# Weights, shift rows and maxima moved ahead in a two-layer graph kernel

## The reference

```
def gat_layer(x, W, att_src, att_dst, bias, src, dst, heads, out_ch, concat):
    h = (x @ W.T).reshape(n, heads, out_ch)
    a_src = jnp.einsum('nhc,hc->nh', h, att_src)
    a_dst = jnp.einsum('nhc,hc->nh', h, att_dst)
    e = jax.nn.leaky_relu(a_src[src] + a_dst[dst], NEG_SLOPE)
    m = jax.ops.segment_max(e, dst, num_segments=n)
    ex = jnp.exp(e - m[dst])
    denom = jax.ops.segment_sum(ex, dst, num_segments=n)
    ... # out = sum over edges of ex / denom * h[src], then + bias

def _performer_attn(x, qkv_w, ...):          # q, k, v = x @ qkv_w
    q = _feature_map(q, w_orf); k = _feature_map(k, w_orf)
    D = jnp.einsum('bhnm,bhm->bhn', q, k_sum)[..., None] + EPSILON
    ktv = jnp.einsum('bhnm,bhnc->bhmc', k, v)
    out = jnp.einsum('bhnm,bhmc->bhnc', q, ktv) / D
    return out @ proj_w + proj_b
```

## Time and profile before

| | us |
|---|---|
| median of 3 runs | 3565.2 (3563.28 to 3566.42) |
| the profiled execution | 3567.12 |
| its span | 3565.3 |
| TensorE busy | 2986.9 (84%) |
| VectorE busy | 2337.2 (66%) |
| ScalarE busy | 1492.7 (42%) |
| GpSimd busy | 455.7 (13%) |

### The profile page before, as it was taken

One profiled execution on the slowest core, in us unless ns is written; L12 is line 12 of the kernel. 1 busy time (PEld: TensorE's weight loads), 2 busy tenths in 40 slices (PEclk: granted clock), 3 DMA queues, 4 the chain that ended last, 5 costly groups with the idle time before them and its releaser, 6 DMA issues. The chain is left out here.

```text
span 3565.3 us, 50533 instructions
## 1 busy us (share of the span) xinstructions
PE 2986.9 (84%) x18054; PEld 2541.1 (71%) x18054; DVE 2337.2 (66%) x3813; ACT 1492.7 (42%) x2551; POOL 455.7 (13%) x301
## 2 busy tenths in 40 slices
PE   8799997967999997886888599867999986886695
PEld 4699996745888997775886233356999955775694
DVE  6644443735842544996764887656888657996775
ACT  5564554213112332553142577522546413552245
POOL 0488880200000000000002300000000000000000
PEclk6899999988999998997989699978999987998897
DMA  6232223794212554224131321165111093214211
GB/s 209 58 45 32 22 14 109 221 219 97 75 47 78 178 156 120 72 64 123 42 79 31 91 49 41 45 187 132 33 56 31 26 238 105 59 45 128 63 34 45
DMA packets 252271, 311.68 MB, mean 87 GB/s; under 512 B 97911, under 2 KB 180572, under 8 KB 251438
## 3 DMA queue, kind: packets, MB, share of 16 engines
q1 hardware_dynamic: 177282, 276.77, 28.8%
q0 software_dynamic: 74784, 32.32, 5.2%
HBM read 227.47 MB, written 80.57 MB: 86 GB/s over the span
## 5 line engine op out<-in xcount | busy, mean ns | idle before, releaser
L438 POOL DMA_INDIRECT adj_d<-key_val,key_off x160 | 337.6, 2110 | 184.7 <-issue 159.6
L3067 DVE TENSOR_TENSOR expert_wgel<-expert_gel,expert_wps 128x417 f32<-128x417 f32 (+1 forms) x384 | 202.7, 584 | 56.9 <-PE expert_wps L2992 55.1
L2041 PE MATMUL gat00att_ops<-gat00att_h,gat00att_p 125*125 x1600 | 197.2, 279 | 48.6 <-DVE gat00att_p L2017 48.5
L2041 PE MATMUL gat10att_ops<-gat10att_h,gat10att_p 125*125 x1600 | 197.1, 281 | 46.2 <-DVE gat10att_p L2017 46.2
L2041 PEld LDWEIGHTS gat00att_ops<-gat00att_h,gat00att_p 125*125 125x125 f32 x1600 | 183.0, 189 | 63.0 <-issue 63.0
L2041 PEld LDWEIGHTS gat10att_ops<-gat10att_h,gat10att_p 125*125 125x125 f32 x1600 | 186.2, 194 | 57.4 <-issue 57.4
L3039 ACT ACTIVATE expert_gel<-expert_hps 128x417 f32<-128x417 f32 (+1 forms) x384 | 193.8, 519 | 56.0 <-DVE expert_wgel L3067 46.9
L606 PE MATMUL perf_wide<-y_lo,perf_qk_hi 128*128 128x416 f32 (+1 forms) x432 | 156.9, 363 | 37.2 <-DVE perf_qk_lo L795 30.3
L744 ACT ACTIVATE perf_kphi<-perf_wide,perf_lnm 125x384 f32<-125x384 f32 (+1 forms) x180 | 96.7, 630 | 180.3 <-PE perf_wide L630 173.8
L1200 PE MATMUL fc_ps<-y_lo,fc_w_hi 128*128 128x512 f32 (+1 forms) x432 | 155.3, 360 | 19.4 <-DVE fc_w_lo L1242 19.4
L1344 PE MATMUL fc_ops<-fc_w_hi,fc_x_lo 128*125 128x384 f32 x480 | 163.3, 340 | 7.2 <-DVE fc_w_lo L1392 7.2
(11 more groups left out here) (484 smaller groups left out, 8187.1 us busy)
## 6 DMA issues: line engine op xcount, KB each, us to landing
fc_w<-in_L_mix_fc_w SPq DMA_DIRECT2D x96, 384.0 KB
adj_d<-edge_zero SPq DMA_DIRECT2D x4, 2734.4 KB
gat00proj_adj<-adj_d POOLq DMA_DIRECT2D x20, 546.9 KB, 8.0
gat00att_sh<-shift_d SPq DMA_DIRECT2D x16, 546.9 KB
gat10att_sh<-shift_d SPq DMA_DIRECT2D x16, 546.9 KB
perf_w<-in_L_mix_qkv_w SPq DMA_DIRECT2D x18, 384.0 KB
perf_w<-in_L_mix_W_qkv SPq DMA_DIRECT2D x18, 384.0 KB
attn_d<-perf_o SPq DMA_DIRECT2D x12, 560.0 KB
```

The source lines that it names most:

```text
L438: nc.gpsimd.indirect_dma_start(out=adj_flat[u], out_offset=bass.IndirectOffsetOnAxis(ap=key_off[:, c:c + 1], axis=0), in_=key_val[:, c:c + ...
L2041: ins = pe.matmul(ops[0:TP, u, b, t * w:(t + 1) * w], p[:, s, (t0 + t) * TP:(t0 + t + 1) * TP], h[:, s, bass.ds(hd, 1), :], start=(s == 0 ...
L3067: dve.tensor_tensor(wgel[:, q % W, 0:cn], gel[:, q % 3, 0:cn], wps[:, q % 3, 0:cn], ALU.mult).then_inc(wgel_done, 1)
```

## The change

- *First weights.* The first weight pair of perf0 and perf1 is loaded one stage earlier (`FirstWeights`): in the edge stage behind x, and in gat10proj behind the attention rows, ahead of `tw` and of x's third tile. In the ternary gat10proj the rings of x and w shrink to 3 and 4. In the performer VectorE splits the first weights first, makes the constants next, and puts the split of v between the two sides of `rests`.
- *Moved maxima.* `MaxScan` in perf1 no longer scans head 0 ahead of the first `keep_values`; the heads move round by one place, the last being scanned in the last step, and one head a round is interleaved with `keep_values`.
- *Shifts.* The shift stages are gone. A helper `Shifts` makes, turns, keeps and stores the shifts inside fc2 and at the start of proj1; `FirstShift` loads head 0's shift rows for gat10att within proj1.
- *Own weights.* `OneHeadIn` loads all weight blocks, the bias and the attention rows of gat01proj and gat11proj in the 8-head attention ahead; `w_lo` takes the place of `w`. The mask is loaded at tiles 2 and 4 in place of 4 and 6.
- *Fused sums.* A score is one `tensor_tensor_reduce`, and a_s is signalled by itself, so that the diagonal of a tile is set early.
- *Three groups.* The maxima are taken over tiles 0 to 3 (in pieces of 4, 3 and 3 beside tiles 6, 7 and 8, from a copy in SBUF), tiles 4 to 7, and tiles 8 and 9.

The diff, cut to its core:

```diff
@@ edge_norm_stage, SyncE, behind the loads of x
+                first.load(sp)
@@ performer_stage, SyncE
-                load_qk(0)
-                load_features(0)
...
                 sp.wait_ge(w_split, 1)
                 load_v(0)
+                load_features(0)
@@ performer_stage, VectorE (constants were ahead of all this)
                 split_w(qk_parts, 0)
-                split_features(0)
+                ... memsets, casts of wb
                 if biased:
...
+                rests(0, (0,))
                 split_w(v_parts, 1)
-                rests(0)
+                rests(0, (1,))
+                split_features(0)
...
+                keep_values(0)
                 if scan is not None:
+                    dve.nop().then_inc(scan.scanned, 1)
                     dve.wait_ge(scan.mask_ld, 32)
-                    scan.head(dve, 0, 0, 0)
-                keep_values(0)
@@ performer_stage, pair
-                    hd = i * 3 + 1 + u if scan is not None and not last else None
+                    hd = i * 3 + u if scan is not None else None
...
-                                scan.head(dve, i * 3 + 3, 0, i * 3 + 3)
-                            keep_values(i + 1)
+                                scan_beside_values(i * 3 + 2, i + 1)
+                            else:
+                                keep_values(i + 1)
@@ proj_stage, SyncE
                 load_tiles(x, x_d, x_ld, 0)
+                if shifts is not None:
+                    shifts.store(sp)
...
+                if first is not None:
+                    sp.wait_ge(shifts.stored, 16)
+                    first.load(sp)
                 for to, src_d in ahead:
                     move_rows(sp, to, src_d, ahead_ld)
@@ fc2_stage: SyncE, TensorE, VectorE
+                    if i == 18:
+                        shifts.store(sp)
+                    if i == 12:
+                        shifts.turn(pe)
+                    if i == 8:
+                        shifts.make(dve)
+                    if i == 15:
+                        shifts.keep(dve)
@@ gat_project_stage
+    xs, ws = (XS, WS) if ternary is None else (XS - 1, WS - 1)
...
                         move_rows(sp, att[:, 1, :], row_bcast(adst_d, TP), att_ld)
+                        if first is not None:
+                            first.load(sp)
@@ gat_attend_stage, SyncE
-                load(0, 0)
+                if first is None:
+                    load(0, 0)
                 for t in range(NT):
                     move_rows(sp, h[:, t]..., h_ld[t])
                 load(1, 1)
+                ahead.load(sp)
+class OneHeadIn:
+    def load(self, sp):
+        bias_d, w_d, asrc_d, adst_d = self.from_d
+        for kb in range(self.kb_n):
+            sp.dma_start(self.w[:, kb, :], w_d[kb * 128:(kb + 1) * 128, :]).then_inc(self.w_ld, 16)
+        move_rows(sp, self.bias[:], row_bcast(bias_d, TP), self.rows_ld)
+        move_rows(sp, self.att[:, 0, :], row_bcast(asrc_d, TP), self.rows_ld)
+        move_rows(sp, self.att[:, 1, :], row_bcast(adst_d, TP), self.rows_ld)
@@ one_head_project_stage, TensorE, before the products of tile AT = 5 (c order 1, 0 there)
+                    if t == AT:
+                        pe.wait_ge(const_set, 1)
+                        for s in range(FT):
+                            pe.wait_ge(diag_done, s + 1)
+                            spread_tile(hps[:, AT % 2, 0:512], diag, s, rows_done)
@@ one_head_project_stage, ScalarE, in the loop over tiles
+                    if t >= 2:
+                        set_diag(t - 2)
+                    if t == AT:
+                        act.wait_ge(rows_done, FT)
+                        act.copy(first_rows[:], spread_rows(hps[:, AT % 2, 0:512], 0, FT)).then_inc(first_kept, 1)
@@ one_head_project_stage, VectorE
+                def score(t, r, to, done):
+                    dve.tensor_tensor_reduce(halves(prod[:, r, :]), h_tile(t), halves(att[:, r, :]), 1.0, 0.0,
+                                             ALU.mult, ALU.add, to[:, t:t + 1]).then_inc(done, 1)
...
+                    if t == AT + 1:
+                        scan(0, 0, FT, first_rows[:], 0, 4)
+                    if t in (AT + 2, AT + 3):
+                        scan(0, 0, FT, first_rows[:], 4 + (t - AT - 2) * 3, 7 + (t - AT - 2) * 3)
                 terms(NT - 2)
-                dve.wait_ge(mask_ld, 64)
-                scan(0, 0, early)
+                scan(1, FT, early - FT, spread_rows(row, FT, early - FT))
                 terms(NT - 1)
-                scan(1, early, NT - early)
+                scan(2, early, NT - early, spread_rows(row, early, NT - early))
```

370 lines of the change are left out of this document (213 added, 157 removed).

## The result

| | before | changed |
|---|---|---|
| median, us | 3564.24 (3556.06 to 3566.42, 4 runs) | 3466.27 (3461.55 to 3468.70, 4 runs) |
| ratio | | 0.9728, 95% interval 0.9709 to 0.9746 |
| profiled execution, span | 3567.12, 3565.3 | 3468.70, 3466.9 |

The kernel is 98.0 us faster; 91.7 were forecast, and 3473.5 us for the median. Part 1 of the page after shows how little of this is work saved. TensorE is busy 28 us less, with the same 18054 instructions, and VectorE 35 us less than in the earlier trace rows; the rest of the 98 us was waiting.

A forecast was written before the change was run, and what follows sets the result against it. No engine was taken as full (TensorE 84%, VectorE 66%); losses lay at stage starts, shift stages and one-head projections. Terms 5.0 + 4.7 + 23.1 - 4.1 + 21.3 + 12.7 + 29.0 = 91.7 us gave 3473.5, range 3452 to 3502.

The forecast's parts named there:

- perf0: Start of perf0: weights already there, TensorE starts 6.1 us earlier; gain 5.0 us, bounds 0 to 6.2.
- perf1: Start of perf1: earlier weight split and moved scans gain 21.6 us, less 0.3 in the last step: 21.3 (12 to 24).
- Shift stages: gat00shift and gat10shift removed, their work moved into neighbouring stages: gains 4.7 us (4 to 5) and 5.0 us.
- Own weights: gat01proj and gat11proj: tile 0 ends at S+22.3 and S+21.5, gaining 14.1 and 12.2 us; loads hidden in the attentions.
- no more than 13 us of waits for shift rows in gat00att: Sign in the profile after: VectorE waits at most 13 us for shift rows in gat00att, none in gat10att.
- Fused sum: One-head projections: 0.88 us start to start for 768 elements; a tile's terms fall from 4.5 to 2.75 us.
- Rival (b): Fused sum saves nothing on ten tiles of gat11proj and two of gat01proj: 21 us, total 3494; chance 0.09.
- Three groups: Maxima in gat01proj and gat11proj: ten short scans at the end, shifts ready at S+115 and S+100.
- gat10proj: x's third tile queues behind two more weight blocks (2.8 us), ring lets last block out 1.1 later: 4.1 lost (1 to 6).
- the rings: gat10proj: the weight ring of 4 lets the last block out about 1.1 us later, part of the 4.1 lost.
- (c): perf1's weights come late, shared with POOL's mask, and features behind them: 3 to 10 us, total 3480; chance 0.06.
- (d): gat01proj and gat11proj: TensorE's clock at 1.2 GHz throughout, 756 products cost 110 us, total 3583; chance 0.03.

## Why the prediction was right

- **Stage starts.** perf0 5.0 forecast, 4.7 at the first pair and 6.1 by the marks. perf1 21.6 forecast and measured: the term was read off the timeline with the durations of the earlier trace rows, and only the order was new. Over perf1 and proj1 the marks give 36.5 against 34.0. With proj1's first weights as one more mark the profiles split this: perf1 takes 374.0 us (371.6 to 375.9) against 397.3 and 398.4, a gain of 23.9 where 21.3 was forecast, and from there to gat10att's first row it is 115.4 against 128.0, a gain of 12.6 where 12.7 was. So the 2.5 us too few are all perf1's, behind the first pair, where I had 0.3 lost; which of the moved scans brings them no run takes apart, and perf1 scatters by 4.3 us.
- **Shift stages.** 4.7 and 5.0 forecast; 5.4 by the marks for the first. What I priced as one piece is the work, not the stage: an empty one costs 0.73.
- **Own weights.** Right in both parts: tile 0 ends at S+20.5 and S+20.1 in place of S+36.4 and S+33.8, and nothing is paid in the attention, because the loads stand behind the rows that are wanted first. One sign was missed by a little: I had said no more than 13 us of waits for shift rows in gat00att, and the first is 13.79, 5.4 of it at the end of fc2. I took 1.8 and 1.4 us too many for tile 0; its products took 9.7 us, near the fast end of my bounds of 8.2 to 14.9.
- **Fused sum.** 0.88 taken, 0.87 measured. Rival (b) is out. It is worth 19.5 us by the marks, 21 forecast.
- **Three groups.** The shifts were ready at S+113.4 and S+97.9, forecast S+115 and S+100. The grouping itself is worth 5.6 us of that by the marks, most in gat01proj; the early diagonals and the short terms are the rest.
- **gat10proj.** Total right (4.2 lost, 4.1 forecast), but by luck: the rings cost nothing, the added blocks cost 6.0 us and not the 2.8 of their transfer, 2.0 of it by the clock behind the wait, and 1.7 us came back with the slow tile that the kernel before had as well.
- **Rivals (c) and (d).** The v weights were 1.3 us later than forecast, 0.32 us of which VectorE waited. The clock of the steady tiles is 1.00 in both stages, before 1.00 and 0.97, so (d) is out.
- **The queues of perf1.** I held the trace against the Trainium skill ("DMA: Bandwidth & Descriptors", Queues, rings and completion order), by which an engine takes turns between queue rows packet by packet. The runs show that POOL's mask did hold up SyncE's weights, 20 us against 7. But I misread the trace as speaking against the rule. My conclusion from it, v near 2468, was mine and not the page's. In the rows above, 306 packets of GpSimd's queue and 297 of SyncE's go in the same 6 us, a turn for each in the profile's count of packets, and the small ones get a tenth of the bytes. The trace agrees with the rule, and SyncE's late v weights follow from it.
- **What the forecast did not have.** The 6.3 us between 91.7 and 98.0 are, to within a few tenths, perf0 (1.1), the shift stage (0.7), the one-head projections (1.7 and 0.6, with what their marks leave out) and perf1 (2.5). All are sizes; the only term that isn't there at all is gat10proj's for the rings.

## What to carry to other kernels

In a program of stages with barriers, price a stage's start by the first wait on a transfer, and look for a queue earlier in the program that has room behind its urgent rows; what is added ahead of an urgent transfer costs its bytes, and can cost the clock behind the wait besides. A fused operation is worth its time only where its engine sets the pace: the same edit gave 16 us in one stage and 3 in its neighbour. An empty stage costs under 1 us here, so stages are merged for the work in them, not for the barrier.
